# Preparation and latent attention of a decoder layer: two programs in a row, and one program that makes each quad's weights during the quad before it

## The reference

```
c_q = h @ w_q_down                      # h = layernorm(x); 384 columns
q_nope, q_rope = c_q @ w_q_up_nope, c_q @ w_q_up_rope     # 32 heads of 128 and of 64
c_kv, k_rope = h @ w_kv_down, rope(h @ w_k_rope)          # 128 and 64 columns
q_lat = einsum('bhsd,hdr->bhsr', q_nope, wuk)             # wuk, wuv: per head 128 x 128
scores = (q_lat . c_kv + rope(q_rope) . k_rope) / sqrt(192), causal
out = einsum('bhsr,hdr->bhsd', softmax(scores) @ c_kv, wuv) @ w_out
x = x + out
```

## Time and profile before

| what | value |
|---|---|
| time, median of 3 runs | 2244.74 us (2242.34 to 2246.76) |
| the profiled execution | 2247.19 us, its span 2245.4 us |
| PE busy | 2111.0 us of the span, 94% |
| preparation, first attention matmul at | 288.96 us |
| attention's slots | 337.8 to 1748.5 us |
| cross attention and network | the last 496.9 us |

### The profile page before, as it was taken

How to read it: one execution, slowest core, us unless ns; L and a number is a source line. 1 busy time by engine, 2 the same in 40 slices (tenths; PEclk the granted TensorE clock), 3 DMA queues, 4 the chain that set the end, 5 groups by cost and what they waited for, 6 DMA issues and landing times. The chain is left out here.

```text
span 2245.4 us, 31134 instructions
## 1 busy us (share of the span) xinstructions
PE 2111.0 (94%) x10848; PEld 1781.4 (79%) x10848; DVE 1291.9 (58%) x2110; ACT 791.9 (35%) x1900; POOL 705.0 (31%) x416
## 2 busy tenths in 40 slices
PE   5889849999999999999999999999999777999999
PEld 4777638888888888888888888888888556888887
DVE  3666326666666667666666676666666564332321
ACT  3333223434433434334344343343343223232321
POOL 5444333433333434333334343433341004000000
PEclk9899979999999999999999999999999897999999
DMA  6777562211212212227222122121220883021000
GB/s 269 288 251 284 229 232 88 73 56 47 82 40 70 82 36 73 57 95 244 85 70 82 36 74 57 39 82 40 70 82 35 320 339 114 1 76 75 1 38 38
DMA packets 76825, 244.08 MB, mean 109 GB/s; under 512 B 12769, under 2 KB 21985, under 8 KB 72673
## 3 DMA queue, kind: packets, MB, share of 16 engines
q1 hardware_dynamic: 76768, 243.33, 31.8%
HBM read 148.91 MB, written 60.82 MB: 93 GB/s over the span
## 5 line engine op out<-in xcount | busy, mean ns | idle before, releaser
L971 DVE TENSOR_TENSOR at_acc<-at_out,at_acc 128x512 f32<-128x512 f32 x512 | 351.6, 687 | 95.6 <-PE at_out L72 86.8
L70 PE MATMUL at_out<-at_wvo,at_val_hi 128*128 128x512 f32 x1024 | 402.9, 393 | 0.5 <-DVE at_acc L971 0.5
L71 PE MATMUL at_out<-at_wvo,at_val_hi 128*128 128x512 f32 x1024 | 402.7, 393 | 0.0
L72 PE MATMUL at_out<-at_wvo,at_val_lo 128*128 128x512 f32 x1024 | 401.5, 392 | 0.0
L817 ACT ACTIVATE at_probs<-at_probs,at_nmax 128x128 f32<-128x128 f32 x512 | 199.8, 391 | 414.7 <-DVE at_nmax L949 414.7
L866 POOL TENSOR_TENSOR at_probs<-at_probs,at_rsum 128x512 f32<-128x512 f32 x128 | 133.2, 1040 | 444.9 <-DVE at_rsum L954 444.9
L72 PEld LDWEIGHTS at_out<-at_wvo,at_val_lo 128*128 128x128 f32 x1024 | 192.2, 188 | 43.8
L70 PEld LDWEIGHTS at_out<-at_wvo,at_val_hi 128*128 128x128 f32 x1024 | 192.7, 188 | 35.0 <-DVE at_acc L971 1.8
L71 PEld LDWEIGHTS at_out<-at_wvo,at_val_hi 128*128 128x128 f32 x1024 | 192.7, 188 | 32.1
L1521 PE MATMUL ff_lin<-ff_act_hi,ff_w 128*128 128x512 f32 x512 | 201.1, 393 | 6.1 <-DVE ff_act_lo L1456 6.1
L1522 PE MATMUL ff_lin<-ff_act_lo,ff_w 128*128 128x512 f32 x512 | 200.5, 392 | 0.0
(11 more groups left out here) (132 smaller groups left out, 4444.7 us busy)
## 6 DMA issues: line engine op xcount, KB each, us to landing
at_qrope<-at_rope_parts SPq DMA_DIRECT2D x512, 64.0 KB, 2.0
at_w_raw<-wh_d SPq DMA_DIRECT2D x32, 1024.0 KB, 5.8
ab_raw<-in_w_heads SPq DMA_DIRECT2D x32, 832.0 KB, 6.6
wh_d<-ab_out SPq DMA_DIRECT2D x32, 704.0 KB, 3.5
cr_ctx_raw<-in_context SPq DMA_DIRECT2D x16, 1024.0 KB, 9.2
tok_d<-pj_pack SPq DMA_DIRECT2D x8, 1536.0 KB, 10.1
at_w_raw<-wh_d SPq DMA_DIRECT2D x32, 384.0 KB, 3.9
at_acc<-in_x SPq DMA_DIRECT2D x4, 2048.0 KB, 9.4
```

The lines of the kernel that those rows point to most:

```text
L70: pe.matmul(out, w_hi, x_hi, start=first, stop=False)
L71: pe.matmul(out, w_hi, x_lo, start=False, stop=False)
L72: return pe.matmul(out, w_lo, x_hi, start=False, stop=last)
L971: dve.tensor_tensor(at, outb[n][:], at, ALU.add).then_inc(added, 1)
```

## The change

`prepare` and `attend` become one program, `transform`. The chunks are prepared in the order 2, 3, 0, 1 (`ORDER`). Chunks 2 and 3 are stored to `tok_d` and later read back for the second group; chunks 0 and 1 stay in `at_tok`. Only 4 heads' query weights and 2 heads' value weights are absorbed during the preparation. The others are absorbed in the first group's quads: `ABSORB` gives for slots 0, 1, 3, 5, 6 and 7 what is made at the slot's end, for heads 2 and 3 of this quad or for the next quad. The products are plain float32 matmuls, one for each tile in the source, straight from the two loaded ring buffers (`ab_raw`), into the two `at_qbank` banks that `latent` and `rope` use; every use is counted in `q_taken`. ACT and DVE cut the results into high and low parts, which go into `at_wabs` and `at_wvo` and are stored to DRAM already cut; the second group loads them so, without ACT or POOL. Tokens are normalised in place, tile by tile, with one buffer `pj_x`; the down weights come in four pieces. `relayout` goes through DRAM: one store, a wait for it, four loads. The core of the difference, first the tables, then SP, PE, and the rest:

```diff
+        AFTER = {"full": 2, "switch": 2, "later": 0, "last": 0}
+        ABSORB = {0: ("B", 2, 0, 0), 1: ("B", 3, 0, 2), 3: ("A", 0, 1, 4), 5: ("B", 0, 1, 6), 6: ("B", 1, 1, 8),
+                  7: ("A", 2, 1, 10)}
...
-                def absorb(j):
-                    n = HPC * c + j
-                    hi, lo = head_hi[j % 2], head_lo[j % 2]
-                    pe.wait_ge(head_lo_done, n + 1)
-                    pe.wait_ge(taken, 3 * n + 1)
-                    for k in range(QT):
-                        ins = three_passes(pe, products[0][:, k * P:(k + 1) * P], hi[:, k * P:(k + 1) * P],
-                                           lo[:, k * P:(k + 1) * P], hi[:, UK:UV], lo[:, UK:UV], True, True)
-                    ins.then_inc(product_ready, 1)
-                    for i in range(2):
...
-                absorb(0)
-                turns(range(4, 8))
-                absorb(1)
-                for m in range(5):
...
-            def relayout(m, c):
-                sp.wait_ge(rope_lo, 2 * (ROPES * m + c + 1))
-                for h in range(QUAD):
-                    for j in range(4):
-                        sp.dma_start(as_f32(qrope[c][j * HALF:(j + 1) * HALF, h, :]),
-                                     as_f32(rope_parts[h * HALF:(h + 1) * HALF, j, :])).then_inc(qrope_in[c], 16)
...
+            def relayout(m, c):
+                sp.wait_ge(rope_lo, 2 * (ROPES * m + c + 1))
+                sp.dma_start(parts_d[c], as_f32(rope_parts[:])).then_inc(parts_out[c], 16)
+                sp.wait_ge(parts_out[c], 16 * (m + 1))
+                of = parts_d[c].rearrange("(h p) j n -> j p h n", h=QUAD)
+                for j in range(4):
+                    sp.dma_start(as_f32(qrope[c][j * HALF:(j + 1) * HALF]), of[j]).then_inc(qrope_in[c], 16)
...
+            def preparation():
...
+                for i in range(N):
+                    slot = i % CPG
+                    if i < N - 1:
+                        for t in range(BPC):
+                            sp.wait_ge(hn_turn_ready, 2 * BPC * i + turn_order(i).index((t, 1)) + 1)
+                            load_x_tile(i + 1, t)
+                    if i == 0:
+                        sp.wait_ge(ab_mm, 2)
+                        load_head(0, 0, 0)
+                        sp.wait_ge(ab_mm, 4)
+                        load_head(0, 1, 1)
+                    if i < CPG:
+                        sp.wait_ge(down_taken, 5 * i + QT)
+                        sp.dma_start(tok_d[slot][:, 0:KT_HI], as_f32(tok[:, slot, 0:KT_HI])).then_inc(cq_out[slot], 16)
+                        sp.wait_ge(kr_lo, i + 1)
+                        sp.wait_ge(kv_lo, i + 1)
+                        sp.dma_start(tok_d[slot][:, KT_HI:PACK],
+                                     as_f32(tok[:, slot, KT_HI:PACK])).then_inc(key_out[slot], 16)
+                    if i == 0:
...
+                        store_wabs(0, 1, 4)
+                        store_wvo(0, 0, 8)
+                        sp.wait_ge(ab_mm, 6)
+                        load_head(0, 2, 0)
+                        sp.wait_ge(ab_mm, 8)
+                        load_head(0, 3, 1)
...
+            def full_quad(q):
+                parts, uses = USES_PREPARED + 12 * q, first_use(q)
+                load_raw_rope(q + 1)
+                sp.wait_ge(ab_mm, parts + 2)
+                load_pair(q + 1, 0, 0)
+                store_wqr(q + 1)
+                sp.wait_ge(ab_mm, parts + 4)
+                load_head(q + 1, 0, 1)
+                store_wvo(q, 1, uses + USE["full"][1] + 3)
+                sp.wait_ge(ab_mm, parts + 6)
+                load_head(q + 1, 1, 0)
+                relayout(q + 1, 0)
+                store_wabs(q + 1, 0, uses + USE["full"][3] + 3)
+                sp.wait_ge(ab_mm, parts + 8)
+                load_pair(q + 1, 1, 1)
+                relayout(q + 1, 1)
+                sp.wait_ge(ab_mm, parts + 10)
+                load_head(q + 1, 2, 0)
+                store_wvo(q + 1, 0, uses + USE["full"][6] + 3)
+                sp.wait_ge(ab_mm, parts + 12)
+                load_head(q + 1, 3, 1)
+                store_wabs(q + 1, 1, uses + USE["full"][7] + 3)
...
+            def later_quad(m, q1):
+                sp.wait_ge(ql_mm, PAIR * (UNITS * m + 2))
+                load_wabs(q1, 0)
+                sp.wait_ge(rope_mm, ROPES * (m + 1))
+                load_wqr(q1)
+                sp.wait_ge(ql_mm, PAIR * (UNITS * m + 4))
+                load_wabs(q1, 1)
+                sp.wait_ge(out_ready, 4 * (STEPS * m + 4))
+                load_wvo(q1, 0)
+                relayout(m + 1, 0)
...
+            def absorb_pair(i, use, taken):
+                for h in range(2):
+                    pe.wait_ge(q_taken, taken + h)
+                    at = h * ITEM_A
+                    for k in range(QT):
+                        ins = pe.matmul(qbank[(use + h) % 2][:, k * P:(k + 1) * P],
+                                        ring[i][:, at + k * P:at + (k + 1) * P],
+                                        ring[i][:, at + UK:at + UK + KVL], start=True, stop=True)
+                    ins.then_inc(ab_mm, 1)
+            def absorb_head(i, use, taken):
+                for n in range(2):
+                    pe.wait_ge(q_taken, taken + n)
+                    pe.matmul(qbank[(use + n) % 2][:], ring[i][:, 0:DV], ring[i][:, DV + n * CH:DV + (n + 1) * CH],
+                              start=True, stop=True).then_inc(ab_mm, 1)
...
+            def preparation():
...
+                    if i:
+                        for j in range(BPC, 2 * BPC):
+                            hn_turn(i, j)
+                        kv_turn(i - 1)
+                    for m in range(QT):
+                        for k in range(KT):
+                            project(i, m, k)
+                        if i == 0 and m < 2:
+                            pe.wait_ge(ring_in[m], 16)
+                            absorb_pair(m, 2 * m, max(2 * m - 1, 0))
+                    if i == 0:
+                        for h in range(2):
+                            pe.wait_ge(ring_in[h], 32)
+                            absorb_head(h, 4 + 2 * h, 3 + 2 * h)
+                    for k in range(KT):
+                        project(i, 3, k)
+                        project(i, 4, k)
+                        if k >= KT - 5 and k < KT - 1 and i < N - 1:
+                            hn_turn(i + 1, k - (KT - 5))
...
             def opening():
...
+                kv_turn(N - 1)
                 for u in range(2):
-                    rope(0, u, 0, 0, u or None, PAIR * u or None)
                     for h in range(PAIR):
-                        latent(0, u, h, 0, h, u + 1, PAIR * u or None)
-                scores(0, 0, 0)
-                scores(0, 1, 0)
+                        latent(u, h, first + 2 + 2 * u + h, first + 1 + 2 * u + h)
+                rope(1, first + 6, first + 5)
+                pe.wait_ge(down_taken, 5 * N)
+                pe.wait_ge(kr_lo, N)
+                scores(0, 0, 0, first + 6)
+                scores(0, 1, 0, first + 6)
                 turn(0, 0)
+                pe.wait_ge(kv_lo, N)
                 values(0, 0, 0)
...
+                if part := absorbed(kind, s):
+                    what, _, ahead, at = part
+                    i = at // 2 % 2
+                    pe.wait_ge(ring_in[i], 16 * (3 * m + 3 + at // 4))
+                    if what == "A":
+                        absorb_pair(i, use[s] + 1, first + use[s])
+                    else:
+                        absorb_head(i, use[s] + 1, first + use[s])
...
-            def cut(k, m):
-                act.wait_ge(weights_in, 16 * (LOADS * m + k + 1))
-                width = weights[k].shape[2]
-                act.activation(weights[k][:, 0], w_raw[:, 0:width], ACT.Copy).then_inc(weights_hi, 1)
...
+            def take_head(h, use, part):
+                for n in range(2):
+                    cols = slice(h % 2 * D + n * CH, h % 2 * D + (n + 1) * CH)
+                    dve.wait_ge(ab_hi, part + n + 1)
+                    dve.tensor_tensor(wvo[h // 2][:, 1, cols], qbank[(use + n) % 2][:], as_f32(wvo[h // 2][:, 0, cols]),
+                                      ALU.subtract).then_inc(q_taken, 1)
...
+                        for j in range(BPC, 2 * BPC):
+                            hn_turn(i, j)
+                        kv_values(i - 1)
+                    for m in range(QT):
+                        query(i, m)
+                        if i == 0 and m < 2:
+                            take_pair(m, 2 * m, 2 * m)
+                        if i < N - 1:
+                            for t in range(2 * m, min(2 * m + 2, BPC)):
+                                moments(i + 1, t)
+                            for t in range(2 * m - 2, min(2 * m, BPC)):
+                                if t >= 0:
+                                    normalise(i + 1, t)
+                    if i == 0:
+                        for h in range(2):
```

(24 more changed lines are left out.)

1058 lines of the change are left out of this document (539 added, 519 removed).

## The result

The changed kernel takes 2213.67 us (median of 4 runs, 2212.09 to 2215.92) against 2243.54 us (2240.83 to 2246.76) for the kernel before, timed beside it: a ratio of 0.9867, 95% interval 0.985 to 0.9884. The prediction said 2215.

The account below looks back on a forecast made before the run. PE was taken to bound the attention's slots, with slack in front of them. Terms: -105.8 us before the first slot, +71.1 absorbed products, +5 extras, sum -29.7; from 2247.19 to 2217.5, median 2215 us, range 2193 to 2242.

Parts of the forecast that it names:

- (1): Start of the preparation: tokens and down weights land and are cut by 22 us, first projection at 22.5 us.
- (2): First chunk: projections 27.5 us, absorbed weights 6.2, turns 1.4, half clock 2, bank waits 1.9; ends at 61.5 us.
- (3): Chunk boundary: 7.9 us from last projection to next chunk's first, 3 us more for lowered clock; normal chunk 40 us.
- (4): SP's queue: third chunk's tokens stand behind 6.4 MB, PE waits 5 us and more; second chunk 48 us, not 40.
- (5): End of the preparation: third chunk 40 us, fourth 38.5 us, last projection ends at 188 us.
- (6): Opening, with ropes, latents and relayout: slot 0's first score 44 us after the last projection, at 232 us.
- the products' price: First group's quads in the slots: query weights of 28 heads and value weights of 30 cost PE 71.1 us.
- Rival (C): Absorbed products: four passes also for 128 columns, 92.9 us instead of 71.1 in the slots; 2240 us, chance 0.07.
- the extras of the slots: Waits in the slots: 3 us in all for the 44 places and 2 us for the change of groups.
- Rival (E): Slots' ends stall as absorbs wait for ring buffers or delay the next turn; 1 us each gives 2257, chance 0.08.
- Rival (D): Preparation not bound by PE: chunks held at 52 us instead of 40, three boundaries cost 36 more; 2251, chance 0.08.
- Rival (B): Better: token queue hidden, clock stays up over the boundaries, slots take nothing extra; 2193 to 2200 us, chance 0.17.

Follow-up runs that it names:

- the filled kernel: Changed kernel plus 16 matmuls of 512 columns that compute nothing, between turns 5 and 6 at each of three boundaries: 2208.84 us, ratio 0.9839.
- both edits: Changed kernel with the rope keys' steps behind the next chunk's turns and the third chunk's token loads ahead on SP's queue: 2187.5 us, ratio 0.9742.

## Why the prediction was right, point by point

The sum came out at -31.6 us against -29.7. It isn't one term that hit; these are the terms, in us (a chunk runs to the first transpose behind its last projection, the fourth to the matmul behind its last projection, at 194.99):

| step | predicted | measured | off by |
|---|---|---|---|
| (1) first projection | 22.5 | 27.93 | +5.4 |
| (2) first chunk | 39 | 42.8 | +3.8 |
| (3), (4) second chunk | 48 | 48.8 | +0.8 |
| (5) third chunk | 40 | 39.0 | -1.0 |
| (5) fourth chunk | 38.5 | 36.4 | -2.1 |
| (6) opening | 44 | 43.0 | -1.0 |
| slots | +76.1 | +67.3 | -8.8 |
| rest | 0 | +0.9 | +0.9 |

**Mis-sized: the start.** Step (1) took DVE's chain to end with the weights at 22 us. Shown: two scalings stretched by 1.29 and 2.52 us beside POOL's cuts, 3.0 us of start. (POOL had the weights' last low part ready at 26.59, not at 22, but PE was still waiting for DVE's cut then.) The trace of before has the sign, in two rows of DVE that the prediction didn't read; four such scalings should take 3.2 us:

```profile
14.59 4.69 DVE L305 TENSOR_SCALAR pj_hn<-pj_x,pj_mv,pj_rstd 128x1024 f32<-128x1024 f32 x4
66.66 6.46 DVE L305 TENSOR_SCALAR pj_hn<-pj_x,pj_mv,pj_rstd 128x1024 f32<-128x1024 f32 x4
```

The other 2.4 us weren't tested. Some of it is scatter: in the kernels above that start in the same way as the changed one, the first projection began at 27.07 to 28.17.

**Mis-sized: the first chunk.** The allowance for bank waits was 1.9 us, the waits are 1.29 + 2.23 = 3.5, and they are shown by the kernel that drops them. Some 1.2 us more is the clock, 0.66 granted in 57 to 60: in the filled kernel, which runs the same first chunk and was granted 1.00 there, it takes 41.6 us instead of 42.8. The last 1.0 us is in no term of the sum. Where step (2) put 2 us of half clock, in the first projection, it was right (0.43 us a matmul up to 31.84, then 0.229).

**Right: the boundary.** 5.6 us to DVE's cut was predicted and measured, and moving the keys' chain took the wait away. From projection to projection it is 8.9 us, not 7.9, because the turns behind the wait run at half clock; in the filled kernel, at full clock, it is 7.9. The clock itself was mis-sized, 3 us a boundary where the fill shows 2.2 and 1.5 for the third and fourth chunk. That is most of the -1.0 and -2.1 in the table.

**Right: the queue.** First tile 29.5 us after the boundary was predicted, 29.4 measured (100.18 less 70.77); PE's wait was put at 5 us and some more, it is 6.46. The order on the queue is shown to be the cause by the kernel that changes it. That the time fits so well is in part luck: the terms written there, 9.6 and 16 us, add up to 25.6, and nothing in it gives the other 3.9. SP came to the keys' store 10.5 us behind the boundary (81.22), and from there to the first tile's landing it took 19 us.

**Right in sum: the opening.** 44 us predicted, 43.0 measured, and PE's last wait is for the second `relayout`, as foreseen. Two errors met: its store was issued 31.5 us after the last projection, not 34.3 (226.46), and store, wait and loads took 11.5 us, not 9.7.

**The gap before.** The prediction says that PE stood still for 17.2 us while the second program loads what the first had stored. The row that it names ends with another load, that of the sine table `at_sin`, an input. In SP's timeline of before the second program's first load is issued at 280.32, 8.6 us into the gap, and the table's at 282.68. This changes no term of the sum.

**Right: the products' price.** 71.1 us predicted, 70.4 by the starts, 69.9 by doubling them. Rival (C), four passes for 128 columns, would have made it 92.9; it is refuted. The rule named beside it, in "FP8 and Floating Point Precision" of the Trainium skill, would want 0.42 us for such a product; the trace has 0.223, and 0.86 for 512 columns, where the rule's 0.96 is nearer. The measurement decides.

**Wrong in sign, small: the extras of the slots.** The prediction added 3 us for the 44 places and 2 us for the change of groups. PE has no wait at any slot's end nor in the change of groups; it is busy throughout:

```profile
238.00:1715.80 1477.80, 1477.80 (x7794) 1245.90 (x7794) 987.33 (x1601) 511.01 (x1540) 296.39 (x253) 1.00 0.42 141
```

In the earlier trace rows it was idle for 2.7 us there. 70.4 - 2.7 = 67.7, and 67.3 is measured. The doubled products, which make PE later still at each bank, wait no more. Rival (E) is refuted by both kernels.

**Rival (D)** said that chunks would be held at 52 us by transfers and the one buffer. The third and fourth, where no tokens are missing, take 39.0 and 36.4 us, and with both edits the second to fourth take 32.7, 33.6 and 30.9. The DMA share is 0.36, half of the 0.71 of the earlier trace rows. Refuted. **Rival (B)** needed the token queue hidden and the clock kept; neither came by itself, both came by the two edits, and that kernel's 2187.5 lies below the 2193 at which (B) ended.

**What hid what.** The errors of +9.2 us in (1) and (2) met -8.8 in the slots and -3.3 in the other chunks and the opening. That the sum came within 2 us, where single terms missed by up to 8.8, is luck. A forecast of the total says little on its terms; only the timeline's fixed points did.

## What to carry to other kernels

Where one engine is full in the long stage, look for the time in front of it: the gain here is idle PE time that went, from the gap between two programs and from the opening behind it, while the moved work costs on the full engine what it costs anywhere. No version here joins the two programs and leaves the absorbed weights in the preparation, so what the joining alone would give is not shown. Put what the next stage needs first on each in-order queue: moving one chain of six small steps on DVE and ACT, and four loads on SP, gave 26 us on top of the large change's 30, and of the waiting that one edit alone took out, nearly half came back at the next wait. A wait costs more than its length where the clock falls with it, so price both.

## What the runs showed of the hardware

- A DVE `TENSOR_SCALAR` of 128x1024 takes 0.81 us alone and 2.10 or 3.33 us when it begins beside a POOL `TENSOR_TENSOR` of 128x1280, which itself takes 3.35 us instead of 2.9 when it begins beside such a scaling.
- 48 matmuls that compute nothing, some 11 us of PE work, left the kernel no slower and by the medians 4.8 us faster, with the clock at 1.00 in the 3 us behind each boundary, where the changed kernel was granted 0.50, 0.55 and 0.79 (from 78, 128 and 167 us).
- The same wait doesn't always bring the clock down. Up to 57 us the program is the same in the changed kernel and in the kernels with later keys, earlier tokens and the fill, with the same wait of 2.2 us; the window 57 to 60 was granted 0.66, 0.64, 1.00 and 1.00. A first chunk therefore ends 1 us earlier or later from one execution to the next, and of the difference between two profiles that much means nothing.
- A float32 product of 128 columns costs 0.223 us, about two passes of 0.106 us and less than the three that a product of cut parts takes.
